# Delta-rule recurrence on one core: fewer constant products on TensorE, and GpSimd's gated tables and decays in another order

## The chip, the cores and the metric

One core of one Trainium2 chip runs the whole kernel. The metric is the device time of one execution in microseconds, given as the median of several runs.

## The reference

The layer is an attention-like block with a recurrence, followed by a feed-forward block with ternary weights. Four sequences of 512 steps pass through 16 heads, so 64 independent recurrences run over 512 steps. Each keeps a state S of 128 x 128. What the recurrence computes, cut from the reference:

```python
def step(St, inp):
    q_t, k_t, v_t, a_t, b_t = inp
    err = jnp.einsum('bhvk,bhk->bhv', St, k_t) - v_t
    St = a_t[..., None] * St - (b_t[..., None] * err)[..., None] * k_t[:, :, None, :]
    o_t = jnp.einsum('bhvk,bhk->bhv', St, q_t)
    return (St, o_t)
```

Before it stand projections with a short convolution, and after it a normalisation, a gate, the output projection and the feed-forward block. The change touches only the recurrence.

## The kernel before

The program has phases one after the other: `projections`, `recurrence`, `attention_out`, `ternary` and `feed_forward`. The recurrence works on **16 chunks of 32 steps**. A chunk has four blocks (n = 0 to 3) of eight steps, and its 64 recurrences are taken as two halves of 32 (hf = 0 and 1). Five engines run lists of instructions written out by hand, tied by counting semaphores; no planner orders them. `over_chunks` puts the first 14 chunks in a hardware loop of two chunks per pass and the last two behind it. The last chunk has `more` = False.

Within a chunk, for every block and half:

- **VectorE** solves the eight steps inside the block (`solve`, lines 1011 to 1035): 14 pairs of small multiplications (L1030) and additions (L1035) with a table `gb[n]` of products of keys. The first L1030 of a block waits for `s_m`, which says that the table has been multiplied by its gates.
- **ScalarE** copies the solved vectors into X (L771), TensorE transposes X (`x_transposes`, L851), ScalarE copies the transposes out (L766), and TensorE multiplies them with the masked key products (`cross`, L904).
- VectorE takes the result (`cross`, L1045, L1047 and L1051) and begins the next block of that half. While one half is on TensorE and ScalarE, the other is on VectorE.
- Between these, TensorE makes key products (L868), Gram products (L859) and transposes of keys for the next chunk. ScalarE copies them out (L786, L777, L766), in an order that is fixed too.

At the end of a chunk comes the **state section** (lines 949 to 964). `state(r)` (L917) adds to the states of a quarter, VectorE evicts it into UT (L1057), and `state_products` (L872 to 879) multiplies the eight states of group j with the keys and queries of the next chunk. VectorE's `start` (lines 996 to 1004) turns each group into first values of W and O. Groups 0 to 3 are half 0, groups 4 to 7 half 1. The order on TensorE is state(0), state(1), groups 0 and 1, state(2), groups 2 and 3, state(3), two `cross` of block 3, groups 4 to 7. Then the next chunk's x_transposes(0, 0) follows.

`busy(bank, count)` (L843 to 846) issues **constant products**: matmuls of a constant tile `warm` (bf16, 128 x 512) into a bank that the next real product overwrites. They compute nothing that is used. `state_products` issues `fill` of them ahead of each group: one in half 0 and two in half 1. Before the first chunk (lines 970 to 971 and 981 to 982) it issues none.

**GpSimd** (`chunk`, lines 724 to 755) does in each chunk:

- `with_gates(c, n)` (L721): the table of block n times the gates ng, seven multiplications. It needs the tables (`s_gb[n]`) and the gates (`s_ngl`), which SyncE loads, and VectorE's solve of block n waits for it.
- `less_v(c, at, hf)` (L712): subtracts v from W of one half. It waits for VectorE's `start` of that half (for half 0 also state(3)).
- `decay(e)` (L705): eight states of UT times their decay `crow`. Decays 0 to 3 use the first load of crow and 4 to 7 the second, which SyncE issues once decay 3 is done (line 610). VectorE's state(r) waits for decays 2r and 2r + 1 (`s_us`).
- the multiplication of X (L740), for which x_transposes of the next block of the same half waits (`s_rs`), and `masked` (L700), for which `cross` waits (`s_gm`).

**SyncE** issues every load in a fixed order (`chunk`, lines 605 to 637). The ones that matter here are the second crow (after decay 3), vt (after both less_v), gb[0] to gb[2], ng (after the last product with ng of the chunk), the keys and queries of the chunk after next, the first crow of the next chunk (after decay 7, line 631), gb[3], and the store of O.

Of the kernel before, what the change touches and what calls it, by code (L numbers as in the profile page):

```python
# [50 lines left out]
def make_identity(nc, pool, ident, sem):  # L51

    nc.gpsimd.memset(ident[:, :], 0.0).then_inc(sem, 1)  # L53
    pool.wait_ge(sem, 1)
    nc.gpsimd.affine_select(out=ident[:, :], in_=ident[:, :], compare_op=ALU.not_equal, fill=1.0,  # L55
                            base=0, pattern=[[-1, P]], channel_multiplier=1).then_inc(sem, 1)
# [411 lines left out]
def recurrence(nc, scr):  # L468
# [17 lines left out]
    with ExitStack() as ctx:  # L486
# [31 lines left out]
        s_crl = m.sem("crl")  # L518
# [8 lines left out]
        s_dp = m.sem("dp")  # L527
# [26 lines left out]
        D_START, D_CH = 10, 32  # L554
        d_cross = lambda n, hf, more: 26 + hf if n == NBL - 1 and more else 2 * n + hf
        D_STATE = [6, 10, 16, 22]
        D_S = [14, 15, 20, 21, 28, 29, 30, 31]
# [104 lines left out]
        def over_chunks(eng, chunk):  # L662

            with eng.Fori(0, NCH // 2 - 1) as i:
                for p in range(2):
                    chunk(i * 2 + p, i, p, True)
            chunk(NCH - 2, NCH // 2 - 1, 0, True)
            chunk(NCH - 1, NCH // 2 - 1, 1, False)

        @block.gpsimd  # L670
        def _(pool):
            tt = nc.gpsimd.tensor_tensor
            make_identity(nc, pool, ident, s_id)
            nc.gpsimd.memset(warm[:, :], 1.0).then_inc(s_id, 1)
            nc.gpsimd.memset(UT[:, :, :], 0.0).then_inc(s_te, 4)
            nc.gpsimd.memset(O[1][:, :, :], 0.0).then_inc(s_os[1], 16)
            nc.gpsimd.memset(X[:, :, :], 0.0).then_inc(s_x, 4)
            nc.gpsimd.memset(tmp[:, :, :], 0.0).then_inc(s_de, 4)

            nc.gpsimd.memset(mask[:, :, :, :], 1.0).then_inc(s_mask, 1)  # L680
            pool.wait_ge(s_mask, 1)

            nc.gpsimd.affine_select(out=mask[:, :, :, :], in_=mask[:, :, :, :], compare_op=ALU.is_ge, fill=0.0, base=0,
                                    pattern=[[0, 2], [-CH, 4], [0, CH]], channel_multiplier=1).then_inc(s_mask, 1)
            pool.wait_ge(s_mask, 2)

            nc.gpsimd.affine_select(out=mask[:, 0, :, :], in_=mask[:, 0, :, :], compare_op=ALU.is_ge, fill=0.0, base=0,
                                    pattern=[[CH, 4], [1, CH]], channel_multiplier=-1).then_inc(s_mask, 1)

            rows = mask[:, 1, :, :].rearrange("p i (n t) -> p i n t", t=BL)  # L690
            nc.gpsimd.affine_select(out=rows, in_=rows, compare_op=ALU.is_ge, fill=0.0, base=BL - 1,
                                    pattern=[[CH, 4], [BL, NBL], [0, BL]], channel_multiplier=-1).then_inc(s_mask, 1)

            def masked(made, w, hf):

                pool.wait_ge(s_te, made + 4)
                for a, steps in enumerate(window(w)):
                    gm = Gm[:, 8 * hf:8 * hf + 8, a, :, steps]
                    by = mask[:, a, :, steps].unsqueeze(1).broadcast_to([P, 8, 4, steps.stop - steps.start])
                    tt(gm, gm, by, ALU.mult).then_inc(s_gm, 1)  # L700

            def decay(e):

                uu = UT[:, 8 * e:8 * e + 8, :]
                tt(uu, uu, crow[:, 8 * (e % 4):8 * (e % 4) + 8, :], ALU.mult).then_inc(s_us, 1)  # L705

            def less_v(c, at, hf):

                pool.wait_ge(s_vl, 16 * c + 16)
                pool.wait_ge(s_de, at + 4)  # L710
                ww = W[:, HALF * hf:HALF * (hf + 1), BL:]
                tt(ww, ww, vt[:, HALF * hf:HALF * (hf + 1), BL:], ALU.subtract).then_inc(s_wv, 1)  # L712

            def with_gates(c, n):

                pool.wait_ge(s_ngl, 16 * (c + 1))
                pool.wait_ge(s_gb[n], 16 * (c + 1))
                for t in range(BL - 1):
                    w = BL - 1 - t
                    pairs = gb[n][:, :, off[t]:off[t] + w]  # L720
                    last = tt(pairs, pairs, ng[:, :, BL * n + t + 1:BL * (n + 1)], ALU.mult)  # L721
                last.then_inc(s_m, 1)

            def chunk(c, i, p, more):
                with_gates(c, 0)
                less_v(c, D_START + D_CH * c - 6, 0)
                pool.wait_ge(s_rl[p], 32 * i + 32)
                if more:
                    pool.wait_ge(s_crl, 32 * c + 16)
                    pool.wait_ge(s_dp, D_START + D_CH * c - 6)  # L730
                    decay(0)
                    decay(1)
                less_v(c, D_START + D_CH * c, 1)
                with_gates(c, 1)
                for n in range(NBL - 1):
                    for hf in range(2):
                        pool.wait_ge(s_tp, T_START + T_CH * c + t_xt(n, hf, more) + 2)
                        xx = X[:, HALF * hf:HALF * (hf + 1), 0:BL * (n + 1)]
                        by = rr[p][:, 0, HALF * hf:HALF * (hf + 1), n + 1:n + 2].broadcast_to([P, HALF, BL * (n + 1)])
                        tt(xx, xx, by, ALU.mult).then_inc(s_rs, 1)  # L740
                        if n == 0:
                            masked(T_START + T_CH * c + t_later(hf, more) + 2, 1, hf)
                            if more:
                                decay(2 + hf)
                        if (n, hf) == (1, 0):
                            with_gates(c, 2)
                        if (n, hf) == (1, 1):
                            with_gates(c, 3)
                if more:
                    pool.wait_ge(s_crl, 32 * c + 32)  # L750
                    pool.wait_ge(s_dp, D_START + D_CH * c)
                    for e in range(4, 8):
                        decay(e)
                    for hf in range(2):
                        masked(T_START + T_CH * c + t_first(hf) + 2, 0, hf)

            pool.wait_ge(s_mask, 4)
            for hf in range(2):
                masked(8 + 2 * hf + 2, 0, hf)
            over_chunks(pool, chunk)  # L760

        @block.scalar
# [67 lines left out]
        def _(pe):  # L830
# [7 lines left out]
            def bank_d(at, j):  # L838

                pe.wait_ge(s_de, at + j + 1)  # L840
                return psD[j % 4]

            def busy(bank, count):  # L843

                for _ in range(count):
                    nc.tensor.matmul(bank[:, :], warm[:, 0:P], warm[:, :], start=True, stop=True)  # L846
# [25 lines left out]
            def state_products(at, d, p, j, by=1, fill=0):  # L872

                bank = bank_d(at, d)
                busy(bank, fill)
                for q in range(8):
                    last = nc.tensor.matmul(bank[:, 64 * q:64 * q + 64].rearrange("p (a t) -> p a t", a=2), UT[:, 8 * j + q, :],  # L877
                                            kq[p][:, :, 8 * j + q, :], start=True, stop=True)
                last.then_inc(s_dp, by)

            def chunk(c, i, p, more):
                at_t, at_d = T_START + T_CH * c, D_START + D_CH * c
# [66 lines left out]
                if more:  # L949
                    x_transposes(NBL - 1, 0)  # L950
                    busy(bank_d(at_d, D_STATE[0]), 4)
                    state(0)
                    x_transposes(NBL - 1, 1)
                    state(1)
                    for r in range(2):
                        pe.wait_ge(s_de, at_d + D_STATE[r] + 4 + 4)
                        for j in (2 * r, 2 * r + 1):
                            state_products(at_d, D_S[j], 1 - p, j, fill=1)
                        state(2 + r)
                    for hf in range(2):  # L960
                        busy(bank_d(at_d, d_cross(NBL - 1, hf, more)), 2)
                        cross(NBL - 1, hf)
                    for j in range(4, 8):
                        state_products(at_d, D_S[j], 1 - p, j, fill=2)

            pe.wait_ge(s_kq[0], 32)
            for j in range(4):
# [13 lines left out]
            for j in range(4, 8):  # L981
                state_products(D_START - D_CH, D_S_FIRST[j], 0, j)
            over_chunks(pe, chunk)

        @block.vector
# [861 lines left out]
```

## Time and profile before

| What | Value |
|---|---|
| median of 3 runs | 3029.47 us (3019.24 to 3034.47) |
| the profiled execution | 3027.24 us |
| its span | 3025.5 us |
| busy: PE, VectorE, ScalarE, GpSimd | 89%, 68%, 39%, 47% of the span |
| mean granted clock of TensorE | 0.962 of full speed |
| constant products (L846) | 716 matmuls, 214.2 us busy |
| GpSimd's gated tables (L721) | 448 multiplications, 330.9 us busy |

The recurrence takes about 1,275 us of the span, from 940 us to 2217 us. In the page's 40 slices of the span, TensorE is busy for 80 to 90% of nearly every slice of it and VectorE for 60 to 80%. The numbers by slice are averages over stages, so they say only that TensorE is nearly always at work; whether its end or another engine's sets the time has to be read from the timelines.

### The profile page before, as it was taken

The page shows a single profiled execution, that of the slowest core. Times are in us where ns is not written, and L with a number is a line of the kernel's source. Part 1 is how long each engine was busy: PE and PEld are TensorE (multiplying, and loading weights), DVE is VectorE, ACT ScalarE, POOL GpSimd, SP SyncE. Part 2 cuts the span into 40 slices and gives each one's busy share as a digit, 9 for nine tenths or more (in the row PEclk, how much of TensorE's full clock was granted, in tenths as well). Part 3 has the DMA queues.
Part 4 walks back from the last instruction along what each step waited for, and adds up shares of the span by engine and source line. Part 5 has one row for each costly group of instructions (what it writes and reads, how often), then busy time and mean ns, then how long its engine had stood idle before and what let it go on. Part 6 is the DMA issues. An engine that isn't in the chain of part 4 may idle for free. (4 is left out here: it accounts for less than half of the span.)

```text
span 3025.5 us, 57383 instructions
## 1 busy us (share of the span) xinstructions
PE 2701.4 (89%) x18370; PEld 2279.9 (75%) x18370; DVE 2054.5 (68%) x5896; ACT 1184.1 (39%) x2305; POOL 1434.1 (47%) x1213
## 2 busy tenths in 40 slices
PE   8999999999995788888898888889837986699999
PEld 6888788888885677777777777777736775588887
DVE  4767768768783676777777777777848894633333
ACT  4454454454542222222222222222237784533333
POOL 2545345355364777777777777777622220000000
PEclk9999999999997998999999999999968998899999
DMA  5564565565648444444444444444244543100000
GB/s 122 140 198 134 163 177 147 159 180 135 185 134 266 181 183 153 169 167 169 165 172 165 172 176 182 183 182 181 93 188 175 220 185 121 70 7 10 12 12 14
DMA packets 412562, 442.27 MB, mean 146 GB/s; under 512 B 122304, under 2 KB 367040, under 8 KB 389568
## 3 DMA queue, kind: packets, MB, share of 16 engines
q1 hardware_dynamic: 412352, 439.63, 43.4%
q8 instruction: 112, 1.84, 0.2%
q14 instruction: 98, 0.80, 0.1%
HBM read 308.91 MB, written 131.14 MB: 145 GB/s over the span
## 5 line engine op out<-in xcount | busy, mean ns | idle before, releaser
L355 PE MATMUL pa_ps<-pa_x_hi,pa_w_hi 128*128 128x512 f32 x1296 | 507.5, 392 | 10.4 <-ACT pa_y L298 6.2
L355 PE MATMUL pa_ps<-pa_x_lo,pa_w_hi 128*128 128x512 f32 x1296 | 505.1, 390 | 0.0
L355 PE MATMUL pa_ps<-pa_x_hi,pa_w_lo 128*128 128x512 f32 x1296 | 504.9, 390 | 0.0
L1030 DVE TENSOR_TENSOR pb_tmp<-pb_gb,pb_ps 128x112 f32<-128x112 f32 (+6 forms) x1792 | 328.2, 220 | 98.7 <-POOL pb_gb L721 88.6
L438 DVE SCALAR_TENSOR_TENSOR pa_cv<-pa_y,pa_taps,pa_cv 128x2048 f32<-128x2048 f32 x144 | 354.8, 2464 | 17.8
L1035 DVE TENSOR_TENSOR pb_ps<-pb_ps,pb_tmp 128x112 f32<-128x112 f32 (+6 forms) x1792 | 331.3, 226 | 6.3 <-DVE pb_tmp L1030 3.1
L721 POOL TENSOR_TENSOR pb_gb<-pb_gb,pb_ng 128x448 f32<-128x448 f32 (+6 forms) x448 | 330.9, 778 | 2.3 <-DMA pb_gb<-scratch_pairs 2.3
L904 PEld LDWEIGHTS pb_ps<-pb_Gm,pb_XT 128*128 128x128 f32 x2048 | 248.7, 196 | 68.9 <-issue 38.6
L355 PEld LDWEIGHTS pa_ps<-pa_x_hi,pa_w_hi 128*128 128x128 f32 x1296 | 243.7, 188 | 69.0 <-ACT pa_y L298 11.1
L705 POOL TENSOR_TENSOR pb_UT<-pb_UT,pb_crow 128x1024 f32<-128x1024 f32 x120 | 280.5, 2361 | 11.9 <-DMA pb_crow<-scratch_crow 11.9
L355 PEld LDWEIGHTS pa_ps<-pa_x_hi,pa_w_lo 128*128 128x128 f32 x1296 | 243.7, 188 | 50.9
L355 PEld LDWEIGHTS pa_ps<-pa_x_lo,pa_w_hi 128*128 128x128 f32 x1296 | 243.8, 188 | 49.8
L904 PE MATMUL pb_ps<-pb_Gm,pb_XT 128*128 128x64 f32 (+1 forms) x2048 | 256.4, 280 | 18.2 <-ACT pb_XT L766 13.0
L877 PEld LDWEIGHTS pb_ps<-pb_kq,pb_UT 128*128 128x128 f32 x2048 | 253.9, 196 | 11.2 <-issue 1.1
L851 PE MATMUL pb_ps<-pb_ident,pb_X 128*128 128x128 f32 x1024 | 144.3, 286 | 124.6 <-ACT pb_X L771 116.1
L877 PE MATMUL pb_ps<-pb_kq,pb_UT 128*128 128x64 f32 x2048 | 248.4, 276 | 0.0
L766 ACT ACTIVATE pb_XT<-pb_ps 128x512 f32<-128x512 f32 x256 | 140.0, 595 | 240.7 <-PE pb_ps L851 240.6
L225 POOL TENSOR_TENSOR pa_o_vt<-pa_av 128x256 f32<-128x256 f32 x16 | 11.6, 725 | 467.4 <-ACT pa_av L318 467.4
L851 PEld LDWEIGHTS pb_ps<-pb_ident,pb_X 128*128 128x128 f32 x1024 | 116.9, 146 | 152.7 <-issue 63.6
L846 PE MATMUL pb_ps<-pb_warm 128*128 128x512 bf16 x716 | 214.2, 394 | 4.6 <-DVE pb_UT L1057 4.6
L1741 DVE SCALAR_TENSOR_TENSOR pe_hid<-pe_ps,all_scales,pe_sil 128x512 f32<-128x512 f32 x64 | 48.1, 751 | 227.8 <-ACT pe_sil L1625 227.8
L771 ACT ACTIVATE pb_X<-pb_ps 128x256 f32<-128x256 f32 x128 | 48.0, 375 | 354.7 <-DVE pb_ps L1035 354.2
(189 smaller groups left out, 5557.1 us busy)
## 6 DMA issues: line engine op xcount, KB each, us to landing
pb_crow<-scratch_crow SPq DMA_DIRECT2D x30, 2048.0 KB, 9.6
pb_gb<-scratch_pairs SPq DMA_DIRECT2D x64, 896.0 KB, 8.4
pa_o_ng<-scratch_beta SPq DMA_DIRECT2D x16, 1024.0 KB, 8.0
scratch_ng<-pa_o_ng SPq DMA_DIRECT2D x16, 1024.0 KB, 4.5
scratch_A<-pa_o_A SPq DMA_DIRECT2D x16, 1024.0 KB, 4.5
scratch_vt<-pa_o_vt SPq DMA_DIRECT2D x16, 1024.0 KB, 4.5
scratch_q<-pa_o_q SPq DMA_DIRECT2D x16, 1024.0 KB, 6.9
scratch_g<-pa_o_g SPq DMA_DIRECT2D x16, 1024.0 KB, 8.0
```

The source lines that it names most:

```text
L355: last = nc.tensor.matmul(out, w[:, mat, k, :], xx[:, k, b * S:(b + 1) * S], start=(k == 0 and n == 0), stop=(k == KT - 1 and n == 2))
L438: nc.vector.scalar_tensor_tensor(out=out, in0=yy[:, :, k:k + S], scalar=tap(k), in1=out, op0=ALU.mult, op1=ALU.add).then_inc(s_tap, 1)
L705: tt(uu, uu, crow[:, 8 * (e % 4):8 * (e % 4) + 8, :], ALU.mult).then_inc(s_us, 1)
L721: last = tt(pairs, pairs, ng[:, :, BL * n + t + 1:BL * (n + 1)], ALU.mult)
L766: nc.scalar.activation(out, psT[j % 2][:, :].rearrange("p (g k) -> p g k", g=4), ACT.Copy).then_inc(s_te, 1)
L846: nc.tensor.matmul(bank[:, :], warm[:, 0:P], warm[:, :], start=True, stop=True)
L851: last = nc.tensor.transpose(bank[:, q * P:(q + 1) * P], src, ident[:, :])
L877: last = nc.tensor.matmul(bank[:, 64 * q:64 * q + 64].rearrange("p (a t) -> p a t", a=2), UT[:, 8 * j + q, :], kq[p][:, :, 8 * j + q, :], ...
L904: last = nc.tensor.matmul(bank[:, 64 * q:64 * q + 32 * kinds].rearrange("p (a i t) -> p a i t", i=4, t=BL), XT[:, g, :], Gm[:, g, 0:kinds, ...
L1030: tt(tmp[:, hs, 0:w], gb[n][:, hs, off[t]:off[t] + w], xs[:, qs, t:t + 1].broadcast_to([P, QUART, w]), ALU.mult).then_inc(s_mul, 1)
L1035: tt(xs[:, qs, t + 1:BL], xs[:, qs, t + 1:BL], tmp[:, hs, 0:w], ALU.add).then_inc(done, by)
L1741: nc.vector.scalar_tensor_tensor(out=hid[e % 2][:, :], in0=ps[2 * (e % 2) + 1][:, :], scalar=scales[:, 1:2], in1=sil[e % 2][:, :], op0=ALU ...
```

## The change

Two edits on TensorE and a new order on GpSimd:

- TensorE: no constant product ahead of the groups 0 to 3, and one instead of two ahead of each of the groups 4 to 7.
- GpSimd: the tables of blocks 0 and 1 are both done at a chunk's beginning, that of block 2 ahead of `less_v` of half 1, and that of block 3 after the X multiplication (1, 0). Decay 4 stands after the X multiplication (1, 1), behind the two waits that were ahead of decays 4 to 7, and decay 5 after the X multiplication (2, 0). Decays 6 and 7 stay at the end.

```diff
             def chunk(c, i, p, more):
                 with_gates(c, 0)
+                with_gates(c, 1)
                 less_v(c, D_START + D_CH * c - 6, 0)
                 pool.wait_ge(s_rl[p], 32 * i + 32)
                 if more:
@@
                     decay(0)
                     decay(1)
+                with_gates(c, 2)
                 less_v(c, D_START + D_CH * c, 1)
-                with_gates(c, 1)
                 for n in range(NBL - 1):
@@
                             if more:
                                 decay(2 + hf)
                         if (n, hf) == (1, 0):
-                            with_gates(c, 2)
-                        if (n, hf) == (1, 1):
                             with_gates(c, 3)
+                        if n + hf == 2 and more:
+                            if n == 1:
+                                pool.wait_ge(s_crl, 32 * c + 32)
+                                pool.wait_ge(s_dp, D_START + D_CH * c)
+                            decay(3 + n)
                 if more:
-                    pool.wait_ge(s_crl, 32 * c + 32)
-                    pool.wait_ge(s_dp, D_START + D_CH * c)
-                    for e in range(4, 8):
+                    for e in (6, 7):
                         decay(e)
@@
                         for j in (2 * r, 2 * r + 1):
-                            state_products(at_d, D_S[j], 1 - p, j, fill=1)
+                            state_products(at_d, D_S[j], 1 - p, j)
                         state(2 + r)
@@
                     for j in range(4, 8):
-                        state_products(at_d, D_S[j], 1 - p, j, fill=2)
+                        state_products(at_d, D_S[j], 1 - p, j, fill=1)
```

## Rows read from the trace of the kernel before

Timelines are merged: start in us from the span's start, duration in us, engine, line, operation, tiles, shape, number of instructions, and in brackets the idle time of the engine before it and what ended it.

**Rows 1.** The page's costliest groups: busy, mean ns, idle before, its main releaser.

```profile
L1030 DVE TENSOR_TENSOR pb_tmp<-pb_gb,pb_ps 128x112 f32<-128x112 f32 (+6 forms) x1792 | 328.2, 220 | 98.7 <-POOL pb_gb L721 88.6
```

**Rows 2.** VectorE's timeline: beginning of solve(2, 0) in a middle chunk.

```profile
1493.67 0.45 DVE L1030 TENSOR_TENSOR pb_tmp<-pb_gb,pb_ps 128x112 f32<-128x112 f32 x2 [4.10 <-POOL pb_gb L721]
```

**Rows 3.** ScalarE's timeline: its copy of X for (2, 0), there and a chunk later.

```profile
1497.08 0.55 ACT L786 ACTIVATE pb_Gm<-pb_ps 128x256 f32<-128x256 f32 x2 [0.34 <-PE pb_ps L868]
1498.02 0.38 ACT L771 ACTIVATE pb_X<-pb_ps 128x256 f32<-128x256 f32 x1 [0.39 <-DVE pb_ps L1035]
...
1574.77 0.38 ACT L771 ACTIVATE pb_X<-pb_ps 128x256 f32<-128x256 f32 x1
```

**Rows 4.** TensorE's timeline: the transposes of X for (2, 0).

```profile
1498.64 1.06 PE L851 MATMUL pb_ps<-pb_ident,pb_X 128*128 128x128 f32 x8 [1.17 <-ACT pb_X L771]
```

**Rows 5.** Stretches: us, busy (instructions) of PE, PEld, VectorE, ScalarE, GpSimd; PEclk; DMA; GB/s.

```profile
949.60:956.60 7.00, 7.00 (x64) 7.00 (x64) 2.46 (x9) 1.06 (x2) 0.00 (x0) 1.00 0.56 170
...
1131.80:1153.00 21.20, 21.20 (x110) 19.42 (x109) 9.60 (x44) 0.38 (x1) 6.43 (x3) 0.59 0.13 51
...
1532.10:1545.00 12.90, 12.90 (x110) 12.01 (x109) 9.45 (x44) 0.38 (x1) 6.45 (x3) 1.00 0.20 83
```

**Rows 6.** VectorE's timeline in a state section: start of group 1, and cross of block 3.

```profile
1524.09 0.23 DVE L1002 TENSOR_TENSOR pb_ps<-pb_ps,pb_rr 128x64 f32<-128x64 f32 x1 [1.13 <-PE pb_ps L877]
...
1538.59 0.75 DVE L1047 TENSOR_TENSOR pb_O<-pb_O,pb_ps 128x256 f32<-128x256 f32 x2
```

**Rows 7.** TensorE's timeline in that state section: ahead of groups 0, 1, 4, 5.

```profile
1520.00 0.38 PE L846 MATMUL pb_ps<-pb_warm 128*128 128x512 bf16 x1 [0.30 <-DVE pb_UT L1057]
...
1521.94 0.38 PE L846 MATMUL pb_ps<-pb_warm 128*128 128x512 bf16 x1
...
1536.41 0.60 PE L846 MATMUL pb_ps<-pb_warm 128*128 128x512 bf16 x2
...
1538.57 0.59 PE L846 MATMUL pb_ps<-pb_warm 128*128 128x512 bf16 x2
```

**Rows 8.** TensorE's timeline before the first chunk: four groups without constant products.

```profile
949.55 7.36 PE L877 MATMUL pb_ps<-pb_kq,pb_UT 128*128 128x64 f32 x64
956.75 1.04 PE L977 MATMUL pb_ps<-pb_ident,pb_Gm 128*64 128x128 f32 x8
```

**Rows 9.** GpSimd's timeline: end of one chunk, beginning and middle of the next.

```profile
1507.17 9.32 POOL L705 TENSOR_TENSOR pb_UT<-pb_UT,pb_crow 128x1024 f32<-128x1024 f32 x4
...
1520.27 5.18 POOL L721 TENSOR_TENSOR pb_gb<-pb_gb,pb_ng 128x448 f32<-128x448 f32 x7
1533.80 1.82 POOL L712 TENSOR_TENSOR pb_W<-pb_W,pb_vt 128x768 f32<-128x768 f32 x1 [8.34 <-DVE pb_UT L1057]
...
1546.16 1.85 POOL L712 TENSOR_TENSOR pb_W<-pb_W,pb_vt 128x768 f32<-128x768 f32 x1 [5.91 <-DVE pb_O L1004]
...
1565.43 5.16 POOL L721 TENSOR_TENSOR pb_gb<-pb_gb,pb_ng 128x448 f32<-128x448 f32 x7
```

**Rows 10.** Loads of crow, 1480 to 1650 us: issues, landing; then ng, issued at 1510.8.

```profile
L582 SPq DMA_DIRECT2D pb_crow<-scratch_crow x5: 333/373/373, 1487.5 to 1644.0; - x5
...
DMA to landing us min/median/max: 7.4/7.9/13.7
...
DMA to landing us min/median/max: 6.7/6.7/6.7
```

**Rows 11.** Timelines of GpSimd and TensorE in the first chunk.

```profile
998.77 0.66 POOL L740 TENSOR_TENSOR pb_X<-pb_X,pb_rr 128x256 f32<-128x256 f32 x1
...
1003.84 1.97 PE L851 MATMUL pb_ps<-pb_ident,pb_X 128*128 128x128 f32 x8 [9.37 <-ACT pb_X L771]
```

**Rows 12.** VectorE's timeline in the last chunk: the two waits for tables.

```profile
2176.32 0.45 DVE L1030 TENSOR_TENSOR pb_tmp<-pb_gb,pb_ps 128x112 f32<-128x112 f32 x2 [0.59 <-POOL pb_gb L721]
...
2189.94 0.45 DVE L1030 TENSOR_TENSOR pb_tmp<-pb_gb,pb_ps 128x112 f32<-128x112 f32 x2 [2.57 <-POOL pb_gb L721]
```

**Rows 13.** TensorE's timeline: the transposes of X for (3, 0).

```profile
1512.62 1.06 PE L851 MATMUL pb_ps<-pb_ident,pb_X 128*128 128x128 f32 x8 [0.70 <-ACT pb_X L771]
```

## The prediction

> **What bounds the kernel now.** Only the recurrence changes. The first view is the page's list of groups: VectorE's first multiplications of a solve have waited 88.6 us for GpSimd's gated tables [rows 1]. Read alone, that is a large prize; the timelines say what it is worth. In a middle chunk VectorE stands 4.10 us before solve(2, 0), since the table of block 2 isn't ready [rows 2]. The other half is under way on TensorE and ScalarE meanwhile, so the question is who waits for the late solve. It is ScalarE's copy of X, and that lost only 0.39 us, because ScalarE was busy with the key products until 1497.63; a chunk later the copy followed the key products without any idle time [rows 3]. TensorE's transposes idled 1.17 us in front of this step [rows 4], most of it the copy itself and the handovers, which stay. So through the blocks the chain is TensorE, ScalarE, TensorE, and most of VectorE's 4.10 us is slack.
>
> In the state section it is plainer. From the cross of block 3 to the next chunk TensorE is busy 12.90 of 12.90 us [rows 5], and VectorE waits for its products, 1.13 us before the start of group 1 [rows 6]. What is taken off TensorE here comes off the chunk.
>
> **Constant products.** With one constant product a group takes 1521.94 - 1520.00 = 1.94 us, with two 1538.57 - 1536.41 = 2.16 us [rows 7]. The second is therefore worth 0.22 us. The last one is worth less, since the weights of the first real product load under it: four bare groups took 956.75 - 949.55 = 7.20 us, 1.80 each [rows 8], so taking it away gives 0.14. Half 0 gives 4 x 0.14 = 0.56 us, all on the path: VectorE's starts wait for these groups, and state(2) and state(3) wait for banks that the starts free, so the whole ladder moves up. Half 1 gives 4 x 0.22 = 0.88. There group 6 needs a bank that VectorE frees with the first of two additions at 1538.59, by 1539.0 [rows 6], while TensorE reached it at 1536.41 + 2 x 2.16 = 1540.7: 1.7 us to spare. TensorE comes 0.56 + 0.44 = 1.0 us sooner and VectorE 0.56, so 1.3 remain. Sum: 1.44 us a chunk, and all chunks but the last have it: **15 x 1.44 = 21.6 us**. Bounds: 0.14 for all eight (16.8 us) and 0.22 for all eight (26.4 us). I take the split, since each half has a row of its own.
>
> The Trainium skill ("TensorE: Matmul & The Clock Gate", section "Back-to-back issue gap") gives about 131 ns as the sustained spacing of matmuls of 512 columns in a stream with weight loads. By it eight constant products would be worth 1.05 us a chunk, an estimate of 15.7 us in all. This trace disagrees, with 0.22 us for the one behind another, and the sum goes by the trace.
>
> **Tables moved forward.** GpSimd ends the table of block 0 at 1525.4 and then stands 8.34 us until VectorE's state(3) lets less_v begin at 1533.80 [rows 9]. The table of block 1 (5.2 us) fits in there, done by 1530.7. The start may even move up: decays 4 and 5 leave the end and free half of 9.32 us [rows 9], and then ng binds, landed at 1510.8 + 6.7 = 1517.5 [rows 10]. Both tables are done by 1528; less_v can begin about 0.6 us sooner than before. Cover: 5 us. The table of block 2 takes the place of the 5.91 us ahead of less_v of half 1 [rows 9]: less_v and two decays end at 1540.3, the table at 1545.5, while VectorE's start of group 7, the releaser at 1546.16, now ends near 1544.7. Less_v comes up to 0.8 us late against its input. Behind it in the queue stand the X multiplication (0, 0) and the masks, and SyncE's load of vt; VectorE waits for it only with the addition of W in half 1, after another whole solve. Nothing sees it, and with table 1 gone from behind less_v all of these come sooner. If that cover went, it would cost its 0.8 us a chunk.
>
> What the moved tables bring where TensorE bounds: ScalarE's 0.39 us [rows 3] in the six chunks behind a loop's return, 2.3 us, and at most 0.1 us in the eight others before the last, 0.8 us. Bounds: 0 and these.
>
> The first chunk is another case: TensorE stood 9.37 us before the transposes (1, 0) [rows 11], for a solve that waited for table 1. With table 1 done early the limit becomes the X multiplication (0, 0) at 998.77, which the same transposes need. It stays in place, since table 2 now stands ahead of it where table 1 stood. So they go from 1003.84 to about 999.7, 4.1 us, bounds 0 and 4.1. In the last chunk TensorE has little to do and VectorE is the chain; its waits of 0.59 and 2.57 us go [rows 12]: 3.2 us, bounds 0 and 3.2. **Tables together: 10.4 us.**
>
> **Decays 4 and 5.** Decay 4 now waits for the second crow among the block steps, and behind it in GpSimd's queue stands the X multiplication (2, 0), needed by the transposes (3, 0) at 1512.62 [rows 13]. The load was issued at 1487.5, after decay 3, and such loads land in 7.4 to 13.7 us [rows 10], at 1501.2 by the worst. A decay of 2.33 and a multiplication of 1.5 us make 1505.1. Cover: 7 us, of which a slightly earlier TensorE takes one or two. State(2) wants decays 4 and 5 later still. On SyncE's queue the second crow moves with decay 3, and the first crow of the next chunk, behind decay 7, can come up to 4.7 us sooner, but stands behind the key loads; behind it are only gb[3] and the store. Cost 0; with the cover gone, 2.33 us a decay.
>
> **Sum.** 21.6 + 10.4 = 32.0 us off the profiled execution's 3027.24: **2995.2 us**, I say 2995. That execution lies 2.2 us under the median of 3029.47.
>
> **The clock.** In the second chunk the stretch from cross to the next chunk took 21.2 us at a mean clock of 0.59, so four fifths of it at 1.2 GHz; the same 110 instructions took 12.9 us at 1.00 elsewhere [rows 5]. What TensorE did there was thin: the two cross products of block 3, then four groups, two constant products ahead of each. One such stretch costs 8.3 us. The runs spread by 15.2 us, which I read as none to two of them. The constant products around the cross products aren't touched. I leave one in the sum and give the range 8 us for it either way.
>
> **Rivals.**
> - *The clock falls oftener* (slower). The constant products go from the section with the thinnest matmuls. Place: the state section. Price: 8.3 us each time. It decides from four further stretches on (32.0 / 8.3 = 3.9): six more give 2995 + 50 = 3045, all fourteen 3111. Against it: bare groups ran 7 us at clock 1.00 before the first chunk [rows 5]. For it: in the low stretch two constant products per group didn't bring the clock back. Chance 10%. The Trainium skill (same page, part 1, "The HAM clock gate") says that the throttled state is the default and activity releases it; by it fewer constant products can only make such stretches likelier, and the bare groups at 1.00 show no fall from that alone.
> - *TensorE wasn't the bound there* (no change). If VectorE or a bank holds the state section at its old length, group 6's bank first, only the tables pay: 3027.2 - 10.4 = 3017, within 0.5%. TensorE's unbroken busy time speaks against it. Chance 12%.
> - *VectorE's wait pays in full* (much faster). If ScalarE and TensorE can follow, 4.1 us come off in 14 chunks in place of 3.1 in all: 2995 - 57 + 3 = 2941. ScalarE's rows speak against it [rows 3]. Chance 6%.
>
> **How the numbers follow.** The forecast has 72%; its own range is 2980 to 3012, from the bounds of the constant products (5 either way), those of the tables (10 the slower way) and a low stretch more or less. The whole range takes in the rival without change, 2978 to 3018, and leaves out the two others and a little of the forecast's ends. About 0.5%, 15 us, is what a measurement of this kernel can tell from no change. Faster by more than that: 72 + 6 = 78%; same 12%; slower 10%.
>
> **What would show it.** In the profile after: groups 0 to 3 without L846 and 1.80 us apart, groups 4 to 7 1.94 apart; 8 x 15 = 120 fewer L846, 596; chunks 1.5 to 1.9 us shorter; VectorE's wait for L721 near 0, its idle time moved to waits for L904; ScalarE's copy of X for (2, 0) right behind the key products; two tables back to back at a chunk's beginning. I am wrong if the mean clock falls below 0.9 in several state sections, if TensorE idles before group 6, or if chunks shrink by 4 us or more.

## The result and the profile after

| | before | after |
|---|---|---|
| median of the runs taken together (20 of each) | 3038.99 us | 3021.53 us |
| lowest and highest | 3019.24 to 3056.22 | 3007.11 to 3037.66 |
| profiled execution, span, mean clock | 3027.24, 3025.5, 0.962 | 3037.66, 3035.9, 0.948 |

The ratio is 0.9943, 95% interval 0.9927 to 0.9958: **17.3 us or 0.57% faster**. The direction was forecast, the size was not: I had said 32 us. 3021.5 also lies above the range's upper end of 3018. Two things stand out at once. The kernel before takes 3039 in 20 runs, not the 3029 of its first three. And the profiled execution of after is its slowest of 20, at the lowest clock (the fastest had a mean clock of 0.960). So the two profiles may be compared by stage, not by span.

From the page of after, lines that answer to [rows 1] and to the table of before:

```profile
PE 2724.4 (90%) x18250; PEld 2309.8 (76%) x18250; DVE 2060.4 (68%) x5896; ACT 1181.8 (39%) x2305; POOL 1437.8 (47%) x1213
...
PEclk9999999999997999998999899989868998899999
...
L721 POOL TENSOR_TENSOR pb_gb<-pb_gb,pb_ng 128x448 f32<-128x448 f32 (+6 forms) x448 | 330.1, 779 | 58.0 <-DMA pb_ng<-scratch_ng 55.9
L1032 DVE TENSOR_TENSOR pb_tmp<-pb_gb,pb_ps 128x112 f32<-128x112 f32 (+6 forms) x1792 | 328.3, 220 | 18.3 <-POOL pb_gb L721 7.0
...
L848 PE MATMUL pb_ps<-pb_warm 128*128 128x512 bf16 x596 | 183.7, 405 | 0.0
```

(The line numbers of the programs of TensorE, ScalarE and VectorE are two higher than before.) The wait of the solves for their tables is down from 88.6 to 7.0 us [rows 1]. There are 120 constant products fewer. GpSimd now waits for the load of ng, as forecast.

The state section of a middle chunk, TensorE's timeline, against [rows 7]:

```profile
1517.29 3.76 PE L879 MATMUL pb_ps<-pb_kq,pb_UT 128*128 128x64 f32 x32 [0.30 <-DVE pb_UT L1059]
1520.97 2.14 PE L919 MATMUL pb_ps<-pb_XT,pb_KT 32*128 32x128 f32 x32
...
1533.12 0.38 PE L848 MATMUL pb_ps<-pb_warm 128*128 128x512 bf16 x1
...
1535.06 0.38 PE L848 MATMUL pb_ps<-pb_warm 128*128 128x512 bf16 x1
...
1540.90 1.04 PE L853 MATMUL pb_ps<-pb_ident,pb_X 128*128 128x128 f32 x8
```

Two bare groups take 1520.97 - 1517.29 = 3.68 us, 1.84 each (forecast 1.80). A group with one constant product takes 1.94, exactly the figure of before, and no wait comes ahead of group 6. VectorE, ScalarE and TensorE at block 2 of that chunk, against [rows 2, 3, 4] (three timelines):

```profile
1493.04 0.43 DVE L1047 TENSOR_TENSOR pb_ps<-pb_ps,pb_rr 128x256 f32<-128x256 f32 x1 [1.33 <-PE pb_ps L906]
...
1494.88 0.55 ACT L788 ACTIVATE pb_Gm<-pb_ps 128x256 f32<-128x256 f32 x2 [0.34 <-PE pb_ps L870]
1495.31 0.39 ACT L773 ACTIVATE pb_X<-pb_ps 128x256 f32<-128x256 f32 x1
...
1495.94 1.06 PE L853 MATMUL pb_ps<-pb_ident,pb_X 128*128 128x128 f32 x8 [0.67 <-ACT pb_X L773]
```

VectorE's wait for a table has become a wait for TensorE's cross. The copy of X stands directly behind the key products, and TensorE's wait went from 1.17 to 0.67 us. GpSimd's timeline, against [rows 9]:

```profile
1515.13 10.30 POOL L721 TENSOR_TENSOR pb_gb<-pb_gb,pb_ng 128x448 f32<-128x448 f32 x14 [2.14 <-DMA pb_ng<-scratch_ng]
1530.51 1.84 POOL L712 TENSOR_TENSOR pb_W<-pb_W,pb_vt 128x768 f32<-128x768 f32 x1 [5.08 <-DVE pb_UT L1059]
...
1536.93 5.16 POOL L721 TENSOR_TENSOR pb_gb<-pb_gb,pb_ng 128x448 f32<-128x448 f32 x7
1542.05 1.84 POOL L712 TENSOR_TENSOR pb_W<-pb_W,pb_vt 128x768 f32<-128x768 f32 x1
...
1568.91 2.36 POOL L705 TENSOR_TENSOR pb_UT<-pb_UT,pb_crow 128x1024 f32<-128x1024 f32 x1 [1.38 <-DMA pb_crow<-scratch_crow]
```

Both tables stand back to back with 5.08 us to spare behind them (forecast: 5). Less_v of half 1 follows table 2 at once, and decay 4 waits 1.38 us for its load, which nobody sees.

So these steps came as written. What the spans say otherwise is in the clock. A **low stretch** is from here on one in which TensorE's granted clock was 1.2 GHz. Windows of the state section, from the first cross of block 3 to the next chunk's transposes (columns as in [rows 5]), the first row an ordinary one, then three of five others, from the profile of after:

```profile
1529.00:1540.90 11.90, 11.90 (x104) 11.56 (x103) 9.26 (x44) 0.38 (x1) 10.39 (x8) 1.00 0.22 89
...
1200.70:1220.00 19.30, 19.30 (x104) 18.71 (x103) 9.32 (x44) 0.38 (x1) 11.58 (x10) 0.60 0.14 55
...
1682.00:1701.40 19.40, 19.40 (x104) 18.78 (x103) 9.38 (x44) 0.38 (x1) 11.59 (x10) 0.60 0.14 55
...
2002.80:2022.10 19.30, 19.30 (x104) 18.69 (x103) 9.35 (x44) 0.38 (x1) 11.57 (x10) 0.60 0.14 55
```

Five of the 15 state sections ran mostly at 1.2 GHz (the two others begin at 1364.7 and 2162.7), each about 7.5 us longer than the ordinary one, at a mean clock of 0.59 to 0.61. That is the sign that I had named for being wrong: a clock below 0.9 in several state sections. The profile of before had one such section [rows 5]. Where such a stretch begins, TensorE's timeline of after shows:

```profile
1681.86 0.60 PE L848 MATMUL pb_ps<-pb_warm 128*128 128x512 bf16 x2
1682.31 1.87 PE L906 MATMUL pb_ps<-pb_Gm,pb_XT 128*128 128x32 f32 x16
1684.01 0.60 PE L848 MATMUL pb_ps<-pb_warm 128*128 128x512 bf16 x2
1684.44 2.26 PE L906 MATMUL pb_ps<-pb_Gm,pb_XT 128*128 128x32 f32 x16
1686.52 0.61 PE L848 MATMUL pb_ps<-pb_warm 128*128 128x512 bf16 x1
1686.92 3.51 PE L879 MATMUL pb_ps<-pb_kq,pb_UT 128*128 128x64 f32 x16
1690.23 0.63 PE L848 MATMUL pb_ps<-pb_warm 128*128 128x512 bf16 x1
```

The first cross takes 1.87 us, the second 2.26: the clock falls inside the **second cross of block 3**, and the groups behind it take 3.7 us in place of 1.94. TensorE hadn't been idle. In before's stretch the second cross took 2.20, in the same place. In after this is so in four of the five sections; in the fifth both crosses took 1.87 us and the fall shows in the constant product right behind the second (0.44 us in place of 0.38). The falls thus come ahead of nearly all the constant products of half 1 that were thinned out, and behind the bare groups of half 0.

### The profile page after: what moved, and what is told of

Same layout as the page of the kernel before. It is cut to its first block and busy times, and to the rows that moved or that the text cites. A ratio compares the mean times of both kernels' runs of the same rounds, so it can differ in the third digit from the quotient of the medians.

```text
span 3035.9 us, 57143 instructions
## 1 busy us (share of the span) xinstructions
PE 2724.4 (90%) x18250; PEld 2309.8 (76%) x18250; DVE 2060.4 (68%) x5896; ACT 1181.8 (39%) x2305; POOL 1437.8 (47%) x1213
## 3 DMA queue, kind: packets, MB, share of 16 engines
q8 instruction: 112, 1.84, 0.2%
## 5 line engine op out<-in xcount | busy, mean ns | idle before, releaser
L906 PEld LDWEIGHTS pb_ps<-pb_Gm,pb_XT 128*128 128x128 f32 x2048 | 256.2, 201 | 67.6 <-issue 37.9
L705 POOL TENSOR_TENSOR pb_UT<-pb_UT,pb_crow 128x1024 f32<-128x1024 f32 x120 | 281.5, 2357 | 22.5 <-DMA pb_crow<-scratch_crow 21.8
L879 PEld LDWEIGHTS pb_ps<-pb_kq,pb_UT 128*128 128x128 f32 x2048 | 273.7, 214 | 11.7 <-DVE pb_UT L1059 7.0
L906 PE MATMUL pb_ps<-pb_Gm,pb_XT 128*128 128x64 f32 (+1 forms) x2048 | 263.4, 285 | 17.2 <-ACT pb_XT L768 13.7
L879 PE MATMUL pb_ps<-pb_kq,pb_UT 128*128 128x64 f32 x2048 | 273.8, 296 | 4.6 <-DVE pb_UT L1059 4.6
L700 POOL TENSOR_TENSOR pb_Gm<-pb_Gm,pb_mask 128x512 f32<-128x512 f32 (+1 forms) x128 | 142.7, 1143 | 124.5 <-ACT pb_Gm L788 124.5
L848 PE MATMUL pb_ps<-pb_warm 128*128 128x512 bf16 x596 | 183.7, 405 | 0.0
```

Of the source, the lines that this page charges most:

```text
L906: last = nc.tensor.matmul(bank[:, 64 * q:64 * q + 32 * kinds].rearrange("p (a i t) -> p a i t", i=4, t=BL), XT[:, g, :], Gm[:, g, 0:kinds, ...
```

## The experiments

Two theories. **A:** the change's own terms are right (about 32 us), and what is missing was lost to low stretches that begin in the two crosses of block 3. **B:** the gain itself is smaller, or the bare and thinned groups cause the falls. "Cross 3" means three constant products ahead of each cross of block 3 where both kernels have two. Results, with the kernel before run in each session (its medians: 3042.78, 3038.77 and 3037.84 us). Across sessions the ratios compare better than the medians:

| run | session | median us (lowest to highest) | ratio to before, 95% |
|---|---|---|---|
| e1_tables | 1 | 3036.02 (3012.94 to 3046.41) | 0.9966 (0.9939 to 0.9992) |
| e2_fills | 1 | 3013.71 (3002.78 to 3022.54) | 0.9912 (0.9879 to 0.9944) |
| e3_after_cross4 | 1 | 3001.23 (2994.19 to 3007.09) | 0.9871 (0.9842 to 0.9900) |
| e4_before_cross4 | 1 | 3040.02 (3035.01 to 3046.15) | 0.9991 (0.9971 to 1.0012) |
| e5_after_again | 2 | 3019.50 (3011.15 to 3028.98) | 0.9941 (0.9915 to 0.9966) |
| e6_after_cross3 | 2 | **2987.98** (2986.03 to 2992.57) | 0.9833 (0.9803 to 0.9863) |
| e7_interleave | 2 | 2998.36 (2993.43 to 3001.97) | 0.9862 (0.9832 to 0.9892) |
| e8_cross4_bare | 2 | 3004.68 (2999.37 to 3009.14) | 0.9884 (0.9853 to 0.9915) |
| e9_before_cross3 | 3 | 3026.61 (3020.74 to 3032.49) | 0.9969 (0.9954 to 0.9985) |
| e10_fills_cross3 | 3 | 3001.84 (3000.24 to 3008.17) | 0.9883 (0.9863 to 0.9902) |
| e11_tables_cross3 | 3 | 3023.17 (3012.02 to 3032.73) | 0.9947 (0.9930 to 0.9964) |
| e12_after_cross1 | 3 | 3062.04 (3044.08 to 3073.41) | 1.0077 (1.0047 to 1.0107) |

**e1_tables**, GpSimd's new order alone: the `chunk` part of the diff, with `fill=1` and `fill=2` left as before.

> GpSimd's new order alone, with the constant products of before. Theory A (the parts are worth what the rows said, and the rest of the forecast's gain is lost to more time at 1.2 GHz behind the two cross products of block 3): 10 us less than before at the same mean clock, about 2 us of it in the chunks of the middle; mean clock as before. Theory B (the moved tables or decays cost something where they now stand): no faster than before, with new waits on GpSimd's L721 or L740 in the chunk.

Measured: 10 us faster by the ratio, as its theory A said, with an interval of 2 to 19. Its profile shows four low stretches of some 20.5 us, so this run says little about the size.

**e2_fills**, TensorE's edit alone:

```diff
-                            state_products(at_d, D_S[j], 1 - p, j, fill=1)
+                            state_products(at_d, D_S[j], 1 - p, j)
@@
-                        state_products(at_d, D_S[j], 1 - p, j, fill=2)
+                        state_products(at_d, D_S[j], 1 - p, j, fill=1)
```

> The constant products of the change alone, with GpSimd's old order. Theory A: a chunk at full clock is 1.45 us shorter than before, but more state sections than before run at 1.2 GHz, mean clock below that of before; net 0 to 12 us less than before. Theory B: 22 us less than before and a mean clock as before.

Measured: 26.8 us faster, more than the whole change and above the 0 to 12 of its theory A; the 22 of its theory B was nearer. Its profile has no low stretch in a state section ahead of the next transposes, only short ones of 3.4 to 10.2 us behind the loop's returns. So the edit of TensorE by itself doesn't bring the falls.

**e3_after_cross4** and **e4_before_cross4**, the same edit on after and on before:

```diff
-                        busy(bank_d(at_d, d_cross(NBL - 1, hf, more)), 2)
+                        busy(bank_d(at_d, d_cross(NBL - 1, hf, more)), 4)
```

> The changed kernel with four instead of two constant products ahead of each cross product of block 3: 4 x 0.22 x 15 = 13 us more work on TensorE. Theory A: the long low stretches that begin there (8.5 us each, five in the changed kernel's profile) vanish, mean clock 0.965 or more, time about 3000 us. Theory B (the low clock has to do with the groups 0 to 3 or 4 to 7 themselves): the low stretches stay, mean clock 0.953, time about 3034 us.

> The kernel before with four instead of two constant products ahead of each cross product of block 3. Theory A: its own long low stretches (20 runs of it lay at 3019 to 3056 us, some two of 8.3 us on the mean) vanish too: about 3019 + 13 = 3032 us with little spread, against 3039. Theory B: 13 us slower than before, 3052, same spread.

Measured: on after, 39.2 us under before, a good 20 us better than the change alone, although it issues 60 more constant products. On before, no gain (3040.0, between the 3032 and the 3052 of the two theories), but the spread of the runs shrank (11 us, against 37 in the first comparison). Neither profile has a long low stretch in a state section. With four on both, after is 38.8 us faster than before: the terms are there in full, against B. The windows of the 14 chunks from the first to the last state section's end, one of each profile:

From after:
```profile
1059.50:2181.60 1122.10, 1009.24 (x9719) 891.94 (x9719) 842.32 (x4116) 286.13 (x672) 811.39 (x731) 0.94 0.44 168
```
From e3_after_cross4:
```profile
1058.60:2136.90 1078.30, 955.65 (x9662) 842.27 (x9774) 842.99 (x4116) 285.24 (x672) 812.25 (x732) 1.00 0.46 175
```

The same work of VectorE, ScalarE and GpSimd, and 43.8 us less time, at a clock of 1.00 in place of 0.94.

**e5_after_again**, the kernel after, unchanged, as the standard of the second session:

> The changed kernel itself once more, beside the three below on one chip, since the products alone (26.8 us faster by its ratio) came out faster than the whole change (17.3). Theory A: the same kernel, about 3021 us, mean clocks 0.951 to 0.958, long low stretches behind the cross products of block 3 in its profile. Rival: the first result was a disturbed one and this gives about 3000 us.

Measured: 3019.50, as in the first comparison; its profile (3014.47 us, clock 0.957) shows four long low stretches.

**e6_after_cross3**: three instead of four.

```diff
-                        busy(bank_d(at_d, d_cross(NBL - 1, hf, more)), 2)
+                        busy(bank_d(at_d, d_cross(NBL - 1, hf, more)), 3)
```

> The changed kernel with three instead of two constant products ahead of each cross product of block 3: 2 x 0.22 x 15 = 6.5 us more work. Theory A: if three are enough to keep the clock, 6 us under the kernel with four (3001 us), about 2995, mean clock 0.97. If the clock needs four: long low stretches remain, 3005 to 3020.

Measured: **2987.98, the fastest of all** (2995 expected), 31.5 us under after and 50.7 us (ratio 0.9833) under before, and its six runs lie within 6.5 us. TensorE's timeline of the same place, from e6_after_cross3:

```profile
1503.75 0.81 PE L848 MATMUL pb_ps<-pb_warm 128*128 128x512 bf16 x3
1504.40 1.87 PE L906 MATMUL pb_ps<-pb_Gm,pb_XT 128*128 128x32 f32 x16
1506.10 0.38 PE L848 MATMUL pb_ps<-pb_warm 128*128 128x512 bf16 x1
1506.32 3.84 PE L879 MATMUL pb_ps<-pb_kq,pb_UT 128*128 128x64 f32 x32
```

The second cross takes 1.87 us, and two groups go by in 3.84 us where the low section of after needed 3.7 for one. (The record of one constant product between those two groups is missing in the trace.)

**e7_interleave**: group 4 is put between the two crosses, on TensorE and VectorE, with no constant product added.

```diff
-        d_cross = lambda n, hf, more: 26 + hf if n == NBL - 1 and more else 2 * n + hf
+        d_cross = lambda n, hf, more: 26 + 2 * hf if n == NBL - 1 and more else 2 * n + hf
@@
-        D_S = [14, 15, 20, 21, 28, 29, 30, 31]
+        D_S = [14, 15, 20, 21, 27, 29, 30, 31]
@@
-                    for j in range(4, 8):
+                        if hf == 0:
+                            state_products(at_d, D_S[4], 1 - p, 4, fill=1)
+                    for j in range(5, 8):
```

> The changed kernel with state group 4 between the two cross products of block 3 on TensorE and VectorE, and no constant product more. Theory A: the two thinnest stretches no longer follow one another, so the clock doesn't fall there; 13 us less work than with four constant products: about 2988 us, mean clock 0.97. Rival: the two thin stretches are not the cause by their being neighbours; low stretches and 3021 us stay.

Measured: no long low stretch in a state section either, without one more product (2998, where 2988 was expected). So parting the two thin crosses does what a further constant product ahead of each does. It is 10.4 us behind e6, with less work on TensorE; its profile shows 3.4 to 10.2 us at 1.2 GHz behind each of the loop's six returns, that of e6 behind two. TensorE's timeline there, from e7_interleave:

```profile
1599.98 1.89 PE L879 MATMUL pb_ps<-pb_kq,pb_UT 128*128 128x64 f32 x16
1604.17 1.11 PE L853 MATMUL pb_ps<-pb_ident,pb_X 128*128 128x128 f32 x4 [2.30 <-issue]
```

**e8_cross4_bare**: four ahead of the crosses as in e3, and none ahead of any group.

```diff
-                        busy(bank_d(at_d, d_cross(NBL - 1, hf, more)), 2)
+                        busy(bank_d(at_d, d_cross(NBL - 1, hf, more)), 4)
@@
-                        state_products(at_d, D_S[j], 1 - p, j, fill=1)
+                        state_products(at_d, D_S[j], 1 - p, j)
```

> The changed kernel with four constant products ahead of each cross product of block 3 and none ahead of any of the eight state groups: 4 x 0.14 x 15 = 8.4 us less work than with one in half 1. Theory A: bare groups keep the full clock once it is there, so 3001 - 8 = 2993 us, clock 0.97. Rival (the constant products of the groups hold the clock): long low stretches return and the time is 3010 us or more.

Measured: 3004.68, not faster than e3, where 8 us were expected. Low stretches are back in four of the 15 sections, but they begin later. From its windows, a low and an ordinary section:

```profile
1436.60:1453.10 16.50, 16.50 (x103) 15.94 (x100) 8.87 (x43) 0.38 (x1) 11.54 (x10) 0.70 0.17 67
...
1361.30:1372.90 11.60, 11.60 (x102) 11.20 (x101) 8.79 (x43) 0.38 (x1) 10.59 (x8) 1.00 0.23 91
```

Here the second cross still took 1.87 us, and the four bare groups 12.06 us. With four products ahead of the crosses, one ahead of each group of half 1 (e3) left no low stretch and none (e8) left four: the rival that I had put on the groups is real with none left in half 1, but not with the change's one.

**e9, e10, e11**: the two edits separately and before itself, all with cross 3; with e6 they make a square. Each is `busy(..., 3)` as in e6, on before (e9), on e2 (e10) and on e1 (e11).

> The kernel before with three instead of two constant products ahead of each cross product of block 3. With it and the next two, the change's two parts are taken apart at a clock that the thin stretch no longer pulls down; the changed kernel with three gave 2988 us. Theory A: no long low stretch, spread of some 10 us, and the forecast's sum of 32 us against the changed kernel with three: about 3020 us (3027 of the forecast's base, less 8.3 for its low stretch, plus 6.5 for the added work is 3025). Rival (the change is worth only the 17 us measured): 3005 us.

> The change's constant products with three ahead of each cross product of block 3, GpSimd's old order. Theory A: 21.6 us under the kernel before with three, 10 us over the changed kernel with three, so about 2998 us. Rival (the order on GpSimd costs what the products alone gained more, 26.8 against 17.3 us): as fast as the changed kernel with three or faster, 2980 to 2988 us.

> GpSimd's new order with three constant products ahead of each cross product of block 3, the state groups' constant products as before. Theory A: 10 us under the kernel before with three, 22 us over the changed kernel with three, so about 3010 us. Rival: no gain over the kernel before with three.

| cross 3 | old order on GpSimd | new order |
|---|---|---|
| old constant products | 3026.61 | 3023.17 |
| new constant products | 3001.84 | 2987.98 |

The constant products give 24.8 us (forecast 21.6). The tables give 3.4 us alone and 13.9 on top of the other edit (forecast 10.4), and both together 38.6 (forecast 32.0). Three of the four come from one session; 2987.98 is from the second, where before stood 0.9 us higher. e11 misses the 3010 of its theory A by 13 us. One pass of the loop, two chunks, measured between transposes at a mean clock of 1.00, in e9, e10 and e6 in this order:

From e9_before_cross3:
```profile
1387.32:1544.08 156.76, 138.98 (x1410) 121.11 (x1410) 119.84 (x588) 41.08 (x96) 115.83 (x104) 1.00 0.46 176
```
From e10_fills_cross3:
```profile
1372.98:1526.96 153.98, 136.11 (x1395) 119.39 (x1394) 119.88 (x588) 41.09 (x96) 115.89 (x104) 1.00 0.47 179
```
From e6_after_cross3:
```profile
1206.73:1359.58 152.85, 135.04 (x1378) 119.36 (x1394) 120.22 (x588) 40.74 (x96) 116.27 (x105) 1.00 0.48 181
```

The passes differ by 2.78 and 1.13 us, but a part of that is the pause at the loop's return, which varies by itself (in e10 from 1.50 to 2.04 us). TensorE's timelines show it inside these three windows:

From e9_before_cross3:
```profile
1466.58 1.09 PE L851 MATMUL pb_ps<-pb_ident,pb_X 128*128 128x128 f32 x8 [1.93 <-issue]
```
From e10_fills_cross3:
```profile
1450.90 1.09 PE L851 MATMUL pb_ps<-pb_ident,pb_X 128*128 128x128 f32 x8 [2.04 <-issue]
```
From e6_after_cross3:
```profile
1284.00 1.09 PE L853 MATMUL pb_ps<-pb_ident,pb_X 128*128 128x128 f32 x8 [1.57 <-issue]
```

With the pause taken off, the constant products give 2.89 us a pass, 1.45 a chunk (forecast 1.44), and the tables 0.66, 0.33 a chunk (forecast 0.22).

Do the tables gain only together with the other edit, as 3.4 against 13.9 suggests? From the first cross of block 3 in the 13th chunk to that in the 15th there are two chunks without a return of the loop, and they ran at a mean clock of 1.00 in all four profiles. They took, in us:

| cross 3 | old order on GpSimd | new order |
|---|---|---|
| old constant products | 153.52 | 152.80 |
| new constant products | 150.62 | 149.83 |

So where the clock held the tables gave 0.72 us in two chunks with the old constant products and 0.79 with the new ones: the two edits add up. What e11 lacks is at the loop's returns. Its profile shows 10.2 us at 1.2 GHz behind four of the six and 3.4 behind the two others, and the passes with the longer ones took 160.2 to 160.5 us, the others 157.0 and 157.1. e9 has one such stretch, e10 and e6 two each. Why e11 has more is open, with one profile each.

**e12_after_cross1**: the other way, one constant product ahead of each cross.

```diff
-                        busy(bank_d(at_d, d_cross(NBL - 1, hf, more)), 2)
+                        busy(bank_d(at_d, d_cross(NBL - 1, hf, more)), 1)
```

> The changed kernel with one instead of two constant products ahead of each cross product of block 3: 6.5 us less work on TensorE. Theory A: the thinner stretch pulls the clock down in more chunks, so it is slower than the changed kernel (3020 us) in spite of the work saved: 3030 us or more, mean clock under 0.95. Rival (the number there doesn't matter, three and four gained by another way): 3014 us, mean clock as in the changed kernel.

Measured: 3062.04, 0.77% slower than before and 40 us above after, though it issues fewer products. A low stretch of 17 us or more in nine of the 15 state sections. The second cross and the group behind it, from TensorE's timeline of e12:

```profile
1533.88 1.87 PE L906 MATMUL pb_ps<-pb_Gm,pb_XT 128*128 128x32 f32 x16
1535.59 0.38 PE L848 MATMUL pb_ps<-pb_warm 128*128 128x512 bf16 x1
1535.80 2.30 PE L906 MATMUL pb_ps<-pb_Gm,pb_XT 128*128 128x32 f32 x16
1537.91 0.61 PE L848 MATMUL pb_ps<-pb_warm 128*128 128x512 bf16 x1
1538.32 3.52 PE L879 MATMUL pb_ps<-pb_kq,pb_UT 128*128 128x64 f32 x16
```

So with after's groups, by the profiles taken: one ahead of each cross gives nine low sections and 3062 us, two give four or five and 3020, three give none and 2988.

## Why the prediction was right and where it was wrong

**What bounds: right.** TensorE's products came off the chunk, 1.45 us for a forecast of 1.44. VectorE's 4.1 us of wait gave almost nothing, as the reading of ScalarE's rows said. The rival "VectorE's wait pays in full" (2941) and the rival "TensorE wasn't the bound" (3017 for the tables alone) both fall by the passes of e9, e10 and e6. That the median came near 3017 is a coincidence: a gain of more than 32 us and a loss to the clock.

**Constant products, 21.6 us: right.** 15 chunks of 1.45 us make 21.8, and the medians with three products ahead of the crosses differ by 24.8, inside the bounds of 16.8 and 26.4; where those 3 us more come from is not shown. Bare groups took 1.84 us, not 1.80, and the groups with one 1.94. Weighed against the 15.7 us that I had estimated from the Trainium skill ("TensorE: Matmul & The Clock Gate", section "Back-to-back issue gap"), the runs side with the row.

**Tables, 10.4 us: about right, somewhat low.** The parts below (4.3, 3.9, and 14 middle chunks of some 0.35) make 13.1 us, near the 13.9 measured on top of the first edit; the 3.4 measured alone has low stretches at the returns in it. The parts: in the first chunk the time from the transposes of L977 (L979 after) at 956.75 to the transposes (1, 0) at 1003.84 was 47.09 us, and is 42.81 (956.42 to 999.23), 4.3 us less for a forecast of 4.1. In the profile of after these transposes wait for the X multiplication, the limit that I had named:

```profile
999.23 1.59 PE L853 MATMUL pb_ps<-pb_ident,pb_X 128*128 128x128 f32 x8 [3.21 <-POOL pb_X L741]
```

The last chunk, from its first transposes to its last cross, went from 46.86 (before) to 42.94 us (after), 3.9 for a forecast of 3.2, though part of both ran at a low clock. In the middle chunks it was 0.33 to 0.40 us in place of 0.22. The term there counted ScalarE's 0.39 us in every second chunk and nearly nothing in the others; TensorE's wait before the transposes of X for (2, 0) fell from 1.17 to 0.67 in the one and from 0.86 to 0.67 in the other, 0.69 for the two. TensorE's timeline of the other chunk:

From before:
```profile
1575.39 1.06 PE L851 MATMUL pb_ps<-pb_ident,pb_X 128*128 128x128 f32 x8 [0.86 <-ACT pb_X L771]
```
From after:
```profile
1571.05 1.07 PE L853 MATMUL pb_ps<-pb_ident,pb_X 128*128 128x128 f32 x8 [0.67 <-ACT pb_X L773]
```

**Decays and covers, 0 us: right.** Both tables had 5.08 us to spare. Decay 4 waited for its load, and the X multiplication behind it in the queue still waited for TensorE, so nothing was held up (GpSimd's timeline of after):

```profile
1572.20 1.53 POOL L741 TENSOR_TENSOR pb_X<-pb_X,pb_rr 128x768 f32<-128x768 f32 x1 [0.93 <-PE pb_ps L853]
```

**The clock: this is the step that failed.** The prediction says "The constant products around the cross products aren't touched. I leave one in the sum and give the range 8 us for it either way", on a base of 3027.24. Two errors are in it. First, the base was a lucky one: one long low stretch in the profile and three runs were taken for the kernel's habit, while 20 runs have a median of 3039. With cross 3 before takes 3026.6; less 15 x 2 x 0.22 = 6.6 us for the added products, it would take 3020 without falls, so its median carries an estimated 19 us of low clock. Second, the number of stretches changed. After without falls is 2988.0 - 6.6 = 2981.4 by the same estimate, so its median of 3021.5 carries 40 us. The profile of e5 (3014.47) bears that out: 33 us over 2981.4, and four long stretches of about 7.5 us make 30 of them. The runs' spread, which I read as none to two stretches, was the warning, and the range held only one more or less. (The bounds that I name for the forecast's own range add up to 3018 at the slow end, not to 3012; the measured median lies above both.) The terms' 38.6 less the 21 us that more falls cost make 17.6, against 17.3 measured. Mechanisms right, then, and the term that was mis-sized is the low clock: 19 and 40 us in place of 8.3 and 8.3.

The first rival, "the clock falls oftener", had the right mechanism and price and the wrong place. I put it on the groups from which constant products were taken. The falls begin in the second cross of block 3 or right behind it, ahead of nearly all of them in half 1. The rival turns the sign from about four further stretches; after has about three more than before, and e12, with nine, is indeed slower than before. The sentence of the Trainium skill that I cited beside it ("TensorE: Matmul & The Clock Gate", part 1, "The HAM clock gate") says that activity releases the clock. The trace agrees in e3, e6 and e12; but no low stretch began in the bare groups of half 0, so where the constant products stand counted here beside how many there are.

**What stays open.** Why after falls oftener than before with identical crosses. The bare groups of half 0 stand ahead of the crosses in after, but e2 has them too and its profile shows no fall in a state section. The new order on GpSimd is in e1, whose profile has four, yet the medians don't blame it alone: by the estimate above e2 carries 18.5 us of low clock (3013.7 against 3001.8 - 6.6) and e1 19.4 (3036.0 against 3023.2 - 6.6, a base with low stretches of its own), both about as before's 19, while after carries 40. So the loss came with the two edits together; why, no run shows. Nor is it settled why four products ahead of the crosses cost more than three. By the ratios the step costs 7 us on before, which the 30 added products at 0.22 us (6.6) explain, but 12 us on after, with intervals too wide to tell the two apart.

## What to carry to other kernels

Constant products are worth having where TensorE's real work is thinnest, and there one more can pay several times its price (6.6 us spent, 31.5 us net gained): count them by place, and try one more and one less ahead of the thinnest matmuls before taking any away elsewhere. A saving on TensorE has to be judged with the clock's falls taken out (look at clock and length of the same stretch in every pass), since falls of 7.5 us each can hide half of it. The same holds for the pause at a loop's return, which differed by half a microsecond between passes of one kernel. And three runs are too few for a base whose runs spread by 37 us; here the wide spread went with the low stretches: 37 us for before with two products ahead of the crosses, 12 with three.

## What the runs showed of the hardware that I had not expected

- TensorE's clock fell to 1.2 GHz in the middle of unbroken busy time (11.90 of 11.90 us in an ordinary section, 19.40 of 19.40 in a low one). Matmuls of 32 columns, 16 in a row, were where it mostly fell, and the groups of 64 columns behind them, with one or two constant products each, didn't bring it back before the next chunk.
- Taking out work made the kernel slower (e12, 30 constant products fewer: +40 us), and adding work made it faster (e6, 30 more: -31.5 us).
- The sign of such a fall can be read from one instruction group: 16 products of 32 columns take 1.87 us, and 1.95 to 2.69 when the clock falls inside them, by where inside.
- A pause of TensorE at the loop's return (1.4 to 2.6 us) was followed by 3.4 to 10.2 us at 1.2 GHz in some variants at every pass (e7, e11) and in others seldom (e9: once).
